# A pre-norm attention and LoRA-MoE layer on eight cores: layer norm's last pass on VectorE, the gating chain on GpSimd, and no layer norm ahead of time

## What is computed

```python
x = x + attn(layernorm(x))        # 16 heads of 128, causal, a linear bias per head (alibi)
x = x + ffn(layernorm(x))

def ffn(x):
    base   = x @ W.T + b
    logits = x @ gate_w.T + gate_b                 # 8 experts
    top, idx = top_k(logits, 2)
    gates  = softmax(top)
    xA     = einsum('nd,erd->ner', x, lora_A)      # rank 16
    delta  = einsum('ner,eor->neo', xA, lora_B)
    return base + sum over the 2 chosen experts of gates * delta
```

## Time and profile before

| what | us |
|---|---|
| median of three runs | 4848.78 |
| lowest and highest of them | 4847.58, 5098.42 |
| the profiled execution's own time | 4879.69 |
| its span on the slowest core (core 1) | 4878.1 |
| spans of the eight cores | 4826.8 to 4878.1 |
| mean granted TensorE clock, core 1 | 0.795 of full speed |

### The profile page before, as it was taken

How to read it: one execution, slowest core, us unless ns; L and a number is a source line. 1 busy time by engine, 2 the same in 40 slices (tenths; PEclk the granted TensorE clock), 3 DMA queues, 4 the chain that set the end, 5 groups by cost and what they waited for, 6 DMA issues and landing times. The chain is left out here.

```text
span 4878.1 us, 65585 instructions; the slowest of 8 cores (4826.8 to 4878.1 us)
## 1 busy us (share of the span) xinstructions
PE 3703.0 (76%) x18452; PEld 1711.5 (35%) x18452; DVE 1826.6 (37%) x5360; ACT 1282.3 (26%) x2670; POOL 110.7 (2%) x210
## 2 busy tenths in 40 slices
PE   3588888888888694767735788888888878947677
PEld 1233343443434242323312334434344333413233
DVE  1233544545445021323222445464554641112223
ACT  5431422323223100121144424242332421001211
POOL 0000000000000001000000000000000000010000
PEclk8667678787887796878866787879888788968778
DMA  3211011011110756111132110101101016451111
GB/s 111 57 18 22 14 18 23 14 22 18 18 23 1 164 162 123 65 56 62 59 100 67 21 27 14 25 15 18 23 14 25 16 42 165 151 109 61 61 60 53
DMA packets 55537, 258.38 MB, mean 53 GB/s; under 512 B 13720, under 2 KB 13984, under 8 KB 34720
## 3 DMA queue, kind: packets, MB, share of 16 engines
q0 software_dynamic: 36464, 119.66, 12.2%
q1 hardware_dynamic: 11824, 84.20, 5.3%
q10 hardware_dynamic: 6912, 50.33, 3.0%
HBM read 273.15 MB, written 67.11 MB: 70 GB/s over the span
## 5 line engine op out<-in xcount | busy, mean ns | idle before, releaser
L851 ACT ACTIVATE prT<-dg,cstt 128x128 bf16<-128x128 f32 (+1 forms) x576 | 216.4, 386 | 1852.1 <-DVE dg L823 1211.3
L812 DVE TENSOR_SCALAR sp<-ps 128x512 f32<-128x512 f32 (+3 forms) x1104 | 631.5, 593 | 14.7 <-PE ps L805 4.8
L805 PE MATMUL ps<-QT,KT 128*128 128x512 bf16 (+3 forms) x1104 | 492.6, 487 | 185.5 <-DVE sp L812 145.5
L1123 PE MATMUL cb<-wf,cT 128*128 128x512 bf16 x2048 | 541.5, 429 | 79.6 <-DMA wf<-wf 77.5
L876 ACT ACTIVATE prT<-sp,cstt 128x128 bf16<-128x128 f32 (+2 forms) x1368 | 579.0, 489 | 17.6 <-DVE sp L812 11.5
L420 PE MATMUL bp<-wo,zTt 128*128 128x512 bf16 x2048 | 473.5, 396 | 85.6 <-DMA wo<-wo 68.4
L632 PE MATMUL pp<-xnT,wv 128*128 128x512 bf16 x2048 | 492.0, 405 | 0.1
L632 PE MATMUL pp<-xnT,wq 128*128 128x512 bf16 x2048 | 470.4, 392 | 0.0
L632 PE MATMUL pp<-xnT,wk 128*128 128x512 bf16 x2048 | 466.9, 390 | 0.0
L743 PE MATMUL pz<-va,prT 128*128 128x129 bf16 x3652 | 392.4, 265 | 27.1 <-ACT prT L876 9.7
L1123 PEld LDWEIGHTS cb<-wf,cT 128*128 128x128 bf16 x2048 | 217.2, 108 | 388.7 <-issue 212.0
(11 more groups left out here) (105 smaller groups left out, 2397.4 us busy)
## 6 DMA issues: line engine op xcount, KB each, us to landing
bx<-x SPq DMA_DIRECT2D x32, 1024.0 KB, 6.6
x2d<-b POOLq DMA_DIRECT2D x32, 1024.0 KB, 8.6
c<-x2d ACTq DMA_DIRECT2D x32, 1024.0 KB, 4.9
out<-co SPq DMA_DIRECT2D x32, 1024.0 KB, 3.9
prT<-x ACTq DMA_DIRECT2D x16, 1024.0 KB, 5.0
prT<-x SPq DMA_DIRECT2D x16, 1024.0 KB, 4.9
wv<-wv POOLq DMA_DIRECT2D x32, 512.0 KB, 5.2
wq<-wq POOLq DMA_DIRECT2D x32, 512.0 KB, 5.2
```

Of the source, the lines that this page charges most:

```text
L805: lambda e, c=c, q0=q0, n=n, bank=bank: e.matmul(psc[bank][:, 0:n], KT[:, c * 128:(c + 1) * 128], QT[:, q0 * 128: q0 * 128 + n], start=Tru ...
L812: lambda e, n=n, bank=bank, buf=buf: e.tensor_scalar(spanb[buf][:, 0:n], psc[bank][:, 0:n], 1024.0, -1024.0, ALU.min, ALU.max),
L851: soff=soff: e.activation(probsT[:, pslot:pslot + min(ncols, 128)], diagb[:, soff:soff + min(ncols, 128)] if ncols == 64 else diagb[:, 0:128],
L1123: lambda e, bi=bi, dc=dc, og=og, bk=bk: e.matmul(b["pb"][bk][:, :], b["xnT2"][bi][:, dc * 128:(dc + 1) * 128], b["wfT"][:, dc * D + og * 5 ...
```

## The change

There are four edits.

1. `_plan_ln` does the apply pass (L600) on DVE as a `tensor_scalar`, and not on ACT. All users wait for DVE's semaphore instead of ACT's. The pairs `(s_dve, ...)` of `ptp_copy` and `vaug_ready` are only written in another way.
2. In the FFN, 18 of the 22 DVE operations of the gating chain move to POOL. DVE keeps the max, two reductions and the reciprocal, ACT the Exp. Each still waits for the one before.
3. The layer norm two tiles ahead is gone. Tiles 0 to 2 still come from `prefix`; for tile 3 and on, load and layer norm are emitted at the head of the tile's own iteration.
4. `fin23` is no longer kept back: groups 2 and 3 are finished at the end of the iteration.

```diff
@@ _plan_ln
-    t8 = pg.op("scalar",
-               lambda e: e.activation(xout_bf[:, :], xin[:, :], AF.Identity,
-                                      bias=cc[:, c0 + 7:c0 + 8],
-                                      scale=cc[:, c0 + 6:c0 + 7]),
-               inc=s_act,
+    t8 = pg.op(eng,
+               lambda e: e.tensor_scalar(xout_bf[:, :], xin[:, :],
+                                         cc[:, c0 + 6:c0 + 7],
+                                         cc[:, c0 + 7:c0 + 8],
+                                         ALU.mult, ALU.add),
+               inc=s_dve,
                waits=[(s_dve, t7)] + list(apply_extra))
@@ _plan_ffn
-    pend_fin = []
     for i in range(NT):
         bi = i % 2
         bi3 = i % 3
-        for _f in pend_fin:
-            _f()
-        pend_fin.clear()
-        t_apply = apply_tok[bi3]
+        if i < len(prefix):
+            ld, t_apply = prefix[i]
+        else:
+            ld = pg.op("scalar",
+                       lambda e, i=i, bi3=bi3: e.dma_start(
+                           b["x2b"][bi3][:, :], x2_d.ap()[i]),
+                       inc=sem["cxl"][bi3], amt=16,
+                       waits=[(s_dve, apply_tok[bi3]),
+                              (s_dve, ev_out[bi3]),
+                              (sem["dsb"][i % 2], b_stores[i])])
+            t_apply = _plan_ln(pg, b["x2b"][bi3], b["xnb"][bi3],
+                               b["xnb"][bi3],
+                               b["cc"], 8 * bi3, sem, (sem["cxl"][bi3], ld),
+                               [(s_pe, xnb_rd[bi3])], eng="vector")
+        apply_tok[bi3] = t_apply
...
-        t = pg.op("vector",
+        t = pg.op("gpsimd",
                   lambda e: e.tensor_scalar(g[:, 8:16], b["gl"][:, :],
                                             g[:, 0:1], None, ALU.is_equal),
-                  inc=s_dve, waits=[(s_dve, t)])
+                  inc=s_pool, waits=[(s_dve, t)])
...
         t = pg.op("vector",
                   lambda e: e.tensor_reduce(g[:, 32:33], g[:, 24:32],
                                             AX.X, ALU.min),
-                  inc=s_dve, waits=[(s_dve, t)])
+                  inc=s_dve, waits=[(s_pool, t)])
...
-        ni = i + 2
-        if i >= 1 and ni < NT:
-            nb3 = ni % 3
-            ld = pg.op("scalar",
...
-            apply_tok[nb3] = _plan_ln(pg, b["x2b"][nb3], b["xnb"][nb3],
...
-                    inc=s_pe, waits=[(s_dve, wv_tok), (s_dve, wts_evac)])
+                    inc=s_pe, waits=[(s_pool, wv_tok), (s_dve, wts_evac)])
...
-        def fin23(fi=i, fbi=bi, fbi3=bi3, fev4=ev4, ffinish=finish_og):
...
-        pend_fin.append(fin23)
+        finish_og(2, False)
+        mm = finish_og(3, False)
```

More of the change, by code:

```diff
@@ L311, in emit_x_load @@
                     inc=sem["dxa"][bb], amt=16,
-                    waits=[(s_act, apply_tok[bb])])
+                    waits=[(s_dve, apply_tok[bb])])
             def emit_ln_tile(i):
@@ L715, in _plan_head @@
                 ptp[:, 0:512]),
-            inc=s_dve, waits=[(s_pe, last_tr)]))
+            inc=s_dve, waits=[(s_pe, last_tr)])
     st["vts_tok"] = last_tr
@@ L768, in emit_z @@
                        inc=s_pe,
-                       waits=[(s_dve, zn), st["ptp_copy"]])
+                       waits=[(s_dve, zn), (s_dve, st["ptp_copy"])])
             st["ztr_tok_pe"][zb] = zt
-            st["ptp_copy"] = (s_dve, pg.op(
+            st["ptp_copy"] = pg.op(
                 "vector",
@@ L775, in emit_z @@
                     ptp[:, 0:128]),
-                inc=s_dve, waits=[(s_pe, zt)]))
+                inc=s_dve, waits=[(s_pe, zt)])
         flush_z()
@@ L921, in _plan_ffn @@
     IOTA = cst[:, CST_IOTA8:CST_IOTA8 + 8]
-    for t0 in range(len(prefix)):
-        apply_tok[t0 % 3] = prefix[t0][1]
-    pend_fin = []
     for i in range(NT):
@@ L981, in _plan_ffn @@
                         lambda e: e.tensor_copy(b["gl"][:, :], b["pgl"][:, 0:8]),
-                        inc=s_dve, waits=[(s_pe, glmm), (s_dve, gl_user)])
+                        inc=s_dve, waits=[(s_pe, glmm), (s_pool, gl_user)])
         xamm = 0
@@ L1081, in _plan_ffn @@
                                             g[:, 37:38], ALU.mult),
-                  inc=s_dve, waits=[(s_dve, t)])
-        t = pg.op("vector",
+                  inc=s_pool, waits=[(s_dve, t)])
+        t = pg.op("gpsimd",
                   lambda e: e.tensor_scalar(g[:, 40:48], g[:, 8:16],
                                             g[:, 37:38], None, ALU.mult),
-                  inc=s_dve, waits=[(s_dve, t)])
-        t = pg.op("vector",
+                  inc=s_pool, waits=[(s_pool, t)])
@@ L1169, in finish_og @@
                       inc=s_pe,
-                      waits=[lora_tok[4]] if (fi == 0 and og == 0) else [])
+                      waits=[lora_tok[4]] if (i == 0 and og == 0) else [])
             m = pg.op("tensor",
@@ L1176, in finish_og @@
                       inc=s_pe,
-                      waits=([(s_dve, fwxa_tok)] if first_delta else []) +
-                            ([lora_tok[3]] if (fi == 0 and og == 0) else []))
+                      waits=([(s_dve, wxa_tok)] if first_delta else []) +
+                            ([lora_tok[3]] if (i == 0 and og == 0) else []))
             ev = pg.op("vector",
-                       lambda e, fbi=fbi, fbi3=fbi3, og=og, bk=bk:
-                       e.tensor_tensor(
-                           b["outb"][fbi][:, og * 512:(og + 1) * 512],
+                       lambda e, bi=bi, bi3=bi3, og=og, bk=bk: e.tensor_tensor(
+                           b["outb"][bi][:, og * 512:(og + 1) * 512],
                            b["pb"][bk][:, :],
-                           b["x2b"][fbi3][:, og * 512:(og + 1) * 512],
-                           ALU.add),
+                           b["x2b"][bi3][:, og * 512:(og + 1) * 512], ALU.add),
                        inc=s_dve,
-                       waits=[(s_pe, m), (sem["dob"][fbi], store_tok[fbi])])
+                       waits=[(s_pe, m), (sem["dob"][bi], store_tok[bi])])
             base_evac[bk] = ev
-            fev4[og] = ev
+            ev4[og] = ev
             return m
@@ L1195, in _plan_ffn @@
         base_chunks(3)
-        def fin23(fi=i, fbi=bi, fbi3=bi3, fev4=ev4, ffinish=finish_og):
-            nonlocal wxa_reader
-            ffinish(2, False)
-            mm = ffinish(3, False)
-            wxa_reader = mm
-            xnT2_rd[fbi] = mm
-            ev_out[fbi3] = fev4[-1]
-            store_tok[fbi] = pg.op("sync",
-                                   lambda e, fi=fi, fbi=fbi: e.dma_start(
-                                       out_d.ap()[seq][fi],
-                                       b["outb"][fbi][:, :]),
-                                   inc=sem["dob"][fbi], amt=16,
-                                   waits=[(s_dve, t_) for t_ in fev4])
-        pend_fin.append(fin23)
-    for _f in pend_fin:
-        _f()
-    pend_fin.clear()
+        finish_og(2, False)
+        mm = finish_og(3, False)
+        wxa_reader = mm
+        xnT2_rd[bi] = mm
+        ev_out[bi3] = ev4[-1]
+        store_tok[bi] = pg.op("sync",
+                              lambda e, i=i, bi=bi: e.dma_start(
+                                  out_d.ap()[seq][i], b["outb"][bi][:, :]),
+                              inc=sem["dob"][bi], amt=16,
+                              waits=[(s_dve, t_) for t_ in ev4])
 def _host_consts():
```

85 lines of the change are left out of this document (38 added, 47 removed).

## The result

| | median | lowest to highest | runs |
|---|---|---|---|
| before | 4981.20 us | 4847.58 to 5202.13 | 10 |
| changed | 4827.79 us | 4752.55 to 4943.72 | 10 |

The ratio of changed to before is 0.9816, with an interval from 0.9798 to 0.9835. Both medians contain runs in which one die had a lower TensorE clock than the other; the ratio leaves those out. A second measurement of the changed kernel, `e10_changed`, gave 0.9809 [0.9792, 0.9827]. The rows of the changed kernel are from that run, on core 6.

The account below looks back on a forecast made before the run. The prediction took TensorE (PE), busy 3703 of 4878 us, as the bound, so only shorter PE waits help. Its terms summed to -67.4 us, 4879.7 to 4812.3, scaled to a median of 4782 us; range 4695 to 5020.

Parts of the forecast that it names:

- layer norm out of the middle: FFN: without the layer norm two tiles ahead, PE's mid-tile wait goes, 9.33 us a tile in 26 tiles, -242.6 us.
- layer norm at the head: FFN tiles 3 to 15: PE's first transposes wait 4.37 us, plus 1.5 us of low clock, in 26 tiles, +152.6 us.
- apply pass in head 0: Head 0, 32 tiles: from L594 to PE takes 1.78 us on DVE instead of 2.70 on ACT, -29.4 us.
- output projection: Prefix tiles: DVE gets 1.23 us more ahead of the eviction PE waits for, twice, +2.5 us, bounds 0 and 4.6.
- gating chain: FFN: 18 POOL steps of 0.45 us make 9.58 us, 1.65 above the two base groups' cover, in 30 tiles, +49.5 us.
- one such difference, 1.5 us a tile: FFN head: clock charge behind the new wait, from 32 base matmuls taking 7.07 or 8.65 us; bounds 0 and 3.2.
- 1 to 3 named as a sign: Sign of being right: PE's wait ahead of L1138 or the copy behind it falls to 1 to 3 us a tile.
- likeliest case: The forecast itself: POOL step of 0.39 to 0.5 us, fast apply pass, 4743 to 4830 us; chance 0.30.
- covered chain: Rival: POOL steps of at most 0.36 us keep the gating chain hidden, -116.9 us, 4733 us; chance 0.28.
- POOL as the bound: Rival: at 0.9 us a POOL step the gating chain leaves PE idle in every tile, 5023 us; chance 0.22.
- twice DVE's time: Rival: gating-chain steps on POOL take 0.58 us, chain +119, in all +2, 4851 us; chance 0.10.
- slow apply pass: Rival: the apply pass takes 2.30 us on DVE, +64 us, 4846 us; chance 0.10.

Follow-up runs that it names:

- e10_changed: The changed kernel as it is, measured a second time, on the same chip as e11; ratio to the kernel before 0.9809.
- e5: Kernel before, with only the block of load and layer norm of tile i + 2 moved behind base groups 2 and 3; ratio 0.9507, median 4609.03 us.
- e11: Changed kernel with the gating chain back on DVE, run beside a repeat of the changed kernel; ratio to the kernel before 0.9742.
- e6: Kernel before, with load and layer norm of tile i + 2 moved behind base groups 2 and 3 and the apply pass on DVE; ratio 0.9447.
- e10: The changed kernel as it is, second measurement, run beside e11; ratio to the kernel before 0.9809.
- e2: Kernel before, with only the 18 gating-chain operations moved from DVE to POOL; ratio 1.0081.
- e1: Kernel before, with only the layer norm's apply pass moved from ACT to DVE; ratio 1.0041.
- e9: e6 with the apply pass of FFN tiles 3 to 15 emitted at the head of its tile, the statistics left in the moved place; ratio 0.9605.
- e7: e6 with the 18 gating-chain operations on POOL as well; ratio to the kernel before 0.9565, median 4637.65 us.
- e8: Changed kernel with 17 of the 18 POOL steps issued twice; ratio to the kernel before 1.0302, median 4996.04 us.

## Why the prediction was right or wrong

| term | forecast | measured | from |
|---|---|---|---|
| layer norm out of the middle | -242.6 | -239 | e5 against before |
| layer norm at the head | +152.6 | +133 | 5.12 x 26, e11 against e6 |
| apply pass in head 0 | -29.4 | -20 | L334, and after |
| output projection | +2.5 | +6 | L420 waiting for L433 |
| gating chain | +49.5 | +32 to +39 | e11 against e10 |
| sum | -67.4 | -88 to -81 | |

The measured ratio of 0.9809 to 0.9816 makes -93 to -89 us. The forecast had the mechanism and the sign of every term; the first was right within 2%.

The step that failed is how the sum was read. It came to -1.4% and was put down, by "about what a measurement of this kernel can tell from no change", as a difference that can't be told from none. The runs tell -1.8% from none with an interval of 0.2% on either side. Behind it, the sum itself was a quarter too small: the terms of the head (+152.6 for +133) and of the gating chain (+49.5 for +32 to +39) were both put too high, and a gain too large in head 0 took back a part of that.

**The head.** The wait was forecast at 4.37 us and is 4.44 (115.5/26). The other term was "one such difference, 1.5 us a tile": it is 1.3. And it was left out that the second group of transposes no longer waits for its copy's free buffer behind evictions: 12.1 us at L952 where 27.8 stood, 0.6 us a tile, 16 us. This is most of the 20 us.

**Head 0.** From L594 to PE it was to be 0.30 + 1.23 + 0.25. The step to the pass is 0.39 (2062.14 - 2061.75), the pass 1.35. The 1.23 came from a bf16 copy, an operation of another kind; it reads PSUM as the float32 row of 1.05 ns does, so that the dear rows read PSUM was no reason to prefer it. The Trainium skill, VectorE: DVE Perf Modes, Mode 2×_2P, has two elements a cycle for float32 in SBUF; the trace agrees in kind, with 1346 ns for 2048 columns, 0.66 ns each with the fixed part of the instruction in it, where the tiles from PSUM take 1.05 without it.

**The output projection.** L420 waits 22.8 us for L433, where it waited 17.2. The group before:

```profile
L420 PE MATMUL bp<-wo,zTt 128*128 128x512 bf16 x2048 | 473.5, 396 | 85.6 <-DMA wo<-wo 68.4 <-DVE b L433 17.2
```

The other kernels with ACT's pass show 16.3 (e5) to 18.8 (e2) there, those with DVE's 20.3 (e1) to 27.2 (e9): about twice the forecast, and small.

**The gating chain.** "I take 0.45" was too much. The chain takes 8.65 us for 9.58, so a step is 0.295 + (8.65 - 6.79)/18 = 0.40 us. With this step the forecast's own sum makes (8.65 - 7.93) x 30 = 21.6 us of wait, and 21.9 were measured: the wait is 23.0/30 = 0.8 us a tile, below the 1 to 3 named as a sign. The 10 to 17 us of slower matmuls stood at nothing in the forecast, so the two errors partly cancel. That the cover of 7.93 us fits is luck. It came from one tile with slow base groups and was used for all 30. In e7, with no wait at the head, PE waits 38.4/30 = 1.28 us and the cover is 7.4; in the changed kernel it is 7.9 in the mean, because the base matmuls behind the head's wait run at a lower clock (8.17 in the tile shown, where PE waits 0.48). In tile 1, which has no wait at its head, the wait is 2.12 us. The timeline of it:

```profile
1920.82 0.27 PE L1133 MATMUL cpw<-idft,cq 128*8 128x128 f32 x1 [2.12 <-POOL cq L1101]
```

So the two costs of this kernel overlap in part: POOL's chain costs 1.35 us a tile in e10, 1.84 in e7.

**The statement.** "A difference of 2% is 97 us, about what a measurement of this kernel can tell from no change" rested on no row. The measurements of the changed kernel have intervals of 0.2% on either side, and a gain of 1.8% is then a clear gain. Half of the chance lay on "within 2%"; read as no change, this is wrong. On the forecast's own sum (-1.4%) and with 4743 to 4830 for its likeliest case, all of that case was faster than the 4848.78 of before, if by less than 2%; the text should have said that such a gain can be told from none.

**The rivals.** The covered chain would have needed a step of at most 0.36 us; it is 0.40, near the 0.39 where 2% begins, and the result is near 2%. POOL as the bound and twice DVE's time (0.58) are out at this size; the e8 run shows what they would have done. The Trainium skill, GPSIMD Engine Reference, Engine selection, puts elementwise work with two inputs at about twice VectorE's time. The trace doesn't agree for 8 columns: with two inputs it is 204 ns on POOL (L1022) for 170 on DVE, 1.2 times. With one input and a per-token scalar it is 312 (L1018) for 230, 1.4 times. The groups of both, POOL in the changed kernel and DVE in e5's timeline:

```profile
L1018 POOL TENSOR_SCALAR cq<-cg,cq 128x8 f32<-128x8 f32 x32 | 10.0, 312 | 796.1 <-DVE cq L1015 796.1
...
L1022 POOL TENSOR_TENSOR cq<-cq,cstt 128x8 f32<-128x8 f32 x32 | 6.5, 204 | 4.7
...
L600 DVE TENSOR_SCALAR prT<-prT 128x2048 bf16<-128x2048 f32 x32 | 43.1, 1346 | 5.9 <-DVE prT L594 5.4
```

```profile
2055.18 0.23 DVE L1009 TENSOR_SCALAR cq<-cg,cq 128x8 f32<-128x8 f32 x1
...
2055.51 0.17 DVE L1013 TENSOR_TENSOR cq<-cq,cstt 128x8 f32<-128x8 f32 x1
```

The slow apply pass is out by its row (1346 ns, not 2300). ACT's part of the layer norm was hidden at the head, as said.

**What stays open.** The terms measured sum to 1 to 12 us less than the whole. They are read from waits and tiles, and by the ratios two of them come out otherwise: e11 is 143 us over e6, where the tiles make 133, and e6 is 29 us below e5, where head 0 and the output projection make 14. What makes up the differences was not found; no experiment here held the granted clock fixed.

## What to carry to other kernels

In lists that run strictly in order, ask first what stands behind a waiting instruction and who needs it: moving a block past the finish of two groups and 32 matmuls, on the same engines, brought 4.9%, more than twice what the whole change did. The apply pass on DVE made the kernel 0.4% slower with the layer norm in the middle of the tile and 0.5% faster with it at the head, so an edit is priced at its place and not by itself. A serial chain hides only up to its cover; beyond it each step is paid, and here the matmuls behind ran slower as well. The fastest kernel of all is e6 (0.9447, 4578.93 us at its best), with the block moved and the apply pass on DVE, and the chain left where it was.

## What the runs showed of the hardware

- A wait of PE of 2.4 us cost 0.9 us more in the work behind it, one of 4.4 us 1.3 us. In the 5 us behind the long one the granted clock was 0.50; in the same work with no wait ahead of it, 0.82 (e6).
- A chained operation on POOL of 8 columns or one takes 190 to 320 ns and starts 0.34 to 0.48 us after the one before; on DVE it is 0.27 to 0.34 us (e5). DVE's reduction starts 0.30 to 0.31 us after the start of the POOL operation that it waits for.
- Where the base matmuls run faster, waits that were covered show up again: the base matmuls of e7 are done in 7.94 us and POOL's chain is then late by 1.29 us, for 0.48 in the changed kernel.
